# One step order in the first attention of a four-layer kernel: the second maximum behind the second scores

## What is computed

```python
x = layernorm(hidden_states) * ln_w + ln_b
q, k, v = x @ Wq + bq, x @ Wk + bk, x @ Wv + bv      # 16 heads of 8 channels
q, k = l2norm(q), l2norm(k)
state = q
for _ in range(2):
    att = softmax(einsum('bqhd,bkhd->bhqk', state, k))
    state = einsum('bhqk,bkhd->bqhd', att, v)
return hidden_states + state @ Wo + bo
```

## Time and profile before

| what | value |
|---|---|
| median of three runs | 1473.08 us |
| span of the profiled execution, first to last instruction | 1467.2 us |
| TensorE / VectorE / ScalarE / GpSimd busy over the span | 89% / 77% / 66% / 51% |
| first scores of k = 0 and of k = 63 start at | 42.97 and 469.35 us of the span |
| mean granted TensorE clock over the span | 0.954 |
| granted clock from 88.73 to 470 us | 0.99 |

### The profile page before, as it was taken

The page is one execution under the profiler, slowest core; times in us unless marked ns, Lnnn a source line. Parts: engine busy times, 40 slices in busy tenths (PEclk is TensorE's granted clock), DMA queues, the critical chain, the costliest instruction groups (busy, mean ns, idle before and its releaser), DMA issues. The chain is left out here.

```text
span 1467.2 us, 34194 instructions
## 1 busy us (share of the span) xinstructions
PE 1305.1 (89%) x12121; PEld 987.2 (67%) x12121; DVE 1130.4 (77%) x3054; ACT 969.6 (66%) x1498; POOL 751.3 (51%) x961
## 2 busy tenths in 40 slices
PE   2899999999998689899927999999999998699997
PEld 1566666666654367899915777777777776588886
DVE  5578889889875667899956888888888776567776
ACT  1688888888886447777723777777777777343441
POOL 4775665787852363799866455455444220101112
PEclk9899999999998779999958999999999999799999
DMA  6000000111111021122121111111111110134353
GB/s 234 18 23 20 22 20 20 28 32 28 31 36 30 8 80 32 56 73 73 58 87 51 49 47 48 46 48 47 49 46 38 39 42 18 26 92 116 80 129 82
DMA packets 84430, 77.20 MB, mean 53 GB/s; under 512 B 18224, under 2 KB 72240, under 8 KB 83888
## 3 DMA queue, kind: packets, MB, share of 16 engines
q1 hardware_dynamic: 80176, 66.73, 17.1%
q0 software_dynamic: 4096, 8.40, 2.0%
HBM read 36.26 MB, written 13.63 MB: 34 GB/s over the span
## 5 line engine op out<-in xcount | busy, mean ns | idle before, releaser
L541 ACT ACTIVATE a_p<-a_ps_s 128x1024 f32<-128x1024 f32 x256 | 258.3, 1031 | 25.1 <-PE a_ps_s L400 22.2
L651 DVE TENSOR_REDUCE a_qt<-a_ps_d 128x2 fp32r<-128x512 f32 x256 | 174.6, 687 | 48.9 <-PE a_ps_d L411 44.9
L1298 DVE TENSOR_REDUCE a_qt<-a_ps_d 128x2 fp32r<-128x512 f32 x256 | 173.3, 688 | 44.9 <-PE a_ps_d L1086 39.9
L822 POOL TENSOR_TENSOR a_rn<-a_ss,a_half 128x16 f32<-128x16 f32 x56 | 162.6, 2920 | 1.3
L1203 ACT ACTIVATE a_pg<-a_ps_s 128x1024 f32<-128x1024 f32 x128 | 125.8, 1024 | 26.8 <-PE a_ps_s L1075 25.4
L418 PE MATMUL a_ps_o<-a_p,a_v 128*32 128x256 f32 x2048 | 129.5, 393 | 3.7 <-ACT a_p L541 3.7
L1086 PE MATMUL a_ps_d<-a_kpad,a_qs 128*128 128x512 f32 x256 | 126.0, 495 | 5.8 <-DVE a_qt L1298 2.7
L411 PE MATMUL a_ps_d<-a_kpad,a_qs 128*128 128x512 f32 x256 | 126.8, 496 | 4.3 <-DVE a_qt L651 2.4
L2300 ACT ACTIVATE f_s<-f_ps_g 128x512 f32<-128x512 f32 x72 | 43.0, 598 | 99.9 <-PE f_ps_g L2246 99.7
L1494 POOL DMA_INDIRECT a_picked<-ys,rows x64 | 67.6, 1056 | 61.8 <-PE a_ps_d L1086 50.8
L418 PEld LDWEIGHTS a_ps_o<-a_p,a_v 128*32 128x32 f32 x2048 | 61.2, 112 | 52.9 <-issue 22.3
(11 more groups left out here) (355 smaller groups left out, 3823.9 us busy)
## 6 DMA issues: line engine op xcount, KB each, us to landing
a_kpad<-a_kc SPq DMA_DIRECT2D x512, 32.0 KB
f_gb<-spread SPq DMA_DIRECT2D x64, 256.0 KB, 5.7
a_kpad<-a_kq SPq DMA_DIRECT2D x256, 32.0 KB, 1.8
f_xin<-xs SPq DMA_DIRECT2D x39, 128.0 KB, 2.1
ys<-f_yout SPq DMA_DIRECT2D x39, 128.0 KB, 2.1
w<-in_w SPq DMA_DIRECT2D x2, 2304.0 KB, 11.4
out_x<-X SPq DMA_DIRECT2D x8, 256.0 KB, 6.8
xs<-f_zero SPq DMA_DIRECT2D x15, 128.0 KB
```

The lines of the kernel that those rows point to most:

```text
L541: nc.scalar.activation(probs[:, u % 2, 2 * c:2 * c + 2, :, :].rearrange("p a b c -> p (a b c)"), ps_s[:, 2 * c:2 * c + 2, :].rearrange("p ...
L651: nc.vector.tensor_reduce(qt2[:, (k - PEAK) % 4, 2 * part:2 * part + 2, SHIFT], bank(k, f"m{part}")[:, :].rearrange("p (a b) -> p a b", b= ...
L822: nc.gpsimd.tensor_tensor(rn[:, part * c:(part + 1) * c], ss[:, part * c:(part + 1) * c], half[:, 0:c], ALU.pow).then_inc(rn_ready, 1)
L1298: nc.vector.tensor_reduce(qt[:, b % 2, GLOBAL, n:n + 2, SHIFT], bank(k, f"m{part}")[:, :].rearrange("p (j s) -> p j s", s=S), AX.X, ALU.ma ...
```

## The change

In the first attention's steps the second scores move up directly behind the attend, ahead of qp and m1. m1 then stands next to m2. xT moves from r = 2 to r = 3, zT from r = 3 to r = 0 of the next batch (so that it serves the same sequences), and both now stand between yT and the attend, with their ScalarE copies between exp 0 and exp 1. The projections and the logits thereby use transposes of their own step. `D_ORDER` and VectorE's order stay as they are, and so do all other stages.

```diff
-    A_ORDER = ("yT", "xT", "T", "zT", "KQ")
+    A_ORDER = ("yT", "xT", "zT", "T", "KQ")
...
-                    "yT": r == 2 and batch(b - 2), "xT": r == 2 and batch(b + 3),
-                    "zT": r == 3 and 0 <= b - 3 < ROUTED}[task]
+                    "yT": r == 2 and batch(b - 2), "xT": r == 3 and batch(b + 3),
+                    "zT": r == 0 and 0 <= b - 4 < ROUTED}[task]
...
+                if a_live(k, "xT"):
+                    pe.wait_ge(z1_ready, b + 4)
+                    wait_a(st, "xT")
+                    transposes(ps_a, lambda t: z1[:, t, :], a_full)
+                if a_live(k, "zT"):
+                    pe.wait_ge(z_new, b - 3)
+                    wait_a(st, "zT")
+                    transposes(ps_a, lambda t: Z[:, ((b - 4) * TPB + t) * D:((b - 4) * TPB + t + 1) * D], a_full)
                 if unit(k - 1) or unit(k - LAST_USE):
...
                     last.then_inc(o_full, 1)
-                if a_live(k, "xT"):
-                    pe.wait_ge(z1_ready, b + 4)
-                    wait_a(st, "xT")
-                    transposes(ps_a, lambda t: z1[:, t, :], a_full)
-                if projects:
-                    pe.wait_ge(a_done, a_count(k - 1, "xT"))
-                    project(st, 0, "qp")
-                maxima(st, 1)
                 if unit(k - SECOND):
                     pe.wait_ge(exp_done, exps_of(k, 1))
                     pe.wait_ge(a_done, a_count(k - 1, "T"))
                     scores(k - SECOND, qs2[:, (k - 1) % 2, S:2 * S])
+                if projects:
+                    pe.wait_ge(a_done, a_count(k, "xT"))
+                    project(st, 0, "qp")
+                maxima(st, 1)
                 maxima(st, 2)
...
-                    pe.wait_ge(a_done, a_count(k - 1, "zT"))
+                    pe.wait_ge(a_done, a_count(k, "zT"))
...
-                if a_live(k, "zT"):
-                    pe.wait_ge(z_new, b - 2)
-                    wait_a(st, "zT")
-                    transposes(ps_a, lambda t: Z[:, ((b - 3) * TPB + t) * D:((b - 3) * TPB + t + 1) * D], a_full)
...
                 if a_live(k, "yT"):
                     copy_a(st, "yT", yT[:, :])
+                if a_live(k, "xT"):
+                    act.wait_ge(a_full, a_count(k, "xT"))
+                    nc.scalar.activation(xT[:, :], ps_a[:, 0:S], ACT.Identity, scale=a["ln_w"][:, 0:1],
+                                         bias=a["ln_b"][:, 0:1]).then_inc(a_done, 1)
+                if a_live(k, "zT"):
+                    copy_a(st, "zT", zT[:, :])
                 if unit(k):
                     exps(st, 1, k, p1)
...
-                        dve.wait_ge(a_full, a_count(k - NG, "xT"))
+                        dve.wait_ge(a_full, a_count(k - 3, "xT"))
```

More of the change, by code:

```diff
@@ L577, in _ @@
                     nc.scalar.copy(ot[:, live], ps_o[:, live]).then_inc(o_copied, 1)
[L578 to L581, removed]
                 if unit(k - SECOND):
@@ L588, in _ @@
                     exps(st, 3, k - SECOND, p2)
-                if a_live(k, "zT"):
-                    copy_a(st, "zT", zT[:, :])
                 if unit(k + NG):
```

## The result

The changed kernel takes 1479.12 us (median of 20 runs, 1471.41 to 1482.16) beside 1471.59 us for the kernel before (median of 20, 1468.0 to 1475.32): a ratio of 1.0046, interval 1.0035 to 1.0056, that is +6.8 us (5.1 to 8.2). The direction is the one forecast; the size is under half of the forecast +14.8, and the median lies 0.9 us under the range. The profiled execution has a span of 1476.0 us, 8.8 above that of before. The 1488 was 14.8 above a median of three runs, 1473.08; over twenty runs the kernel before has 1471.59, so 1.5 us of what 1488 was too high lie in that base.

A forecast was written before the change was run, and what follows sets the result against it. Two nearly equal loops, ScalarE's and the banks', were taken to bound the first attention. +13.1 (nine batches), +2.7 (b = 1 to 3) and -1.0 (routing steps) gave +14.8 on 1473.1: 1488 us, range 1480 to 1494.

The forecast's parts named there:

- two loops: Plain step of the first attention: ScalarE's loop closes at 6.30, the bank loop would at 5.92, 0.38 to spare.
- The rule on modes: TensorE in the first attention: one array turn fewer per step; by this alone the step would lose 0.10.
- rival B: First attention: TensorE's own issue is the bound, so the saved array turn makes it faster, -6, 1467; chance 0.06.
- routing steps: k = 31, and k = 47 in smaller measure: late for another reason, so 0.90 shrinks to about 0.15; 1.0 taken off.
- The step that failed most: r = 3: xT's copy holds exp 1 to 3.04, second scores at 3.19, qp 0.90 later; the step ends 0.90 later.
- the plain step: r = 1: m1 and m2 read in series, 0.68 each, O at 5.14, step 6.16 in place of 6.30, -0.14.
- 3 x (0.90 + 0.27 - 0.28): Batches b = 1 to 3, without lg: r = 3 and r = 2 cost, r = 0 and r = 1 gain; +2.7.
- The start ... and the last two batches: The 12 starting steps that wait for data and the last two batches, without projections: taken at nothing.
- m2's wait for qp's read: r = 3: m2 takes qp's bank, so TensorE stands until 4.94; from m2 to the step's end nothing gets shorter.
- A: Same places, half the size: r = 3 +0.67, yT not late, lg's lateness half absorbed; +8.8 less 1.0, 1481; chance 0.18.
- C: No change: r = 1's gain spreads to more steps, r = 3 half as bad; within 2.9 us of before; chance 0.05.
- D: Worse: VectorE's lateness carries on in routing steps and TensorE's idle costs granted clock; up to 6 more, 1494; chance 0.05.

The follow-up runs named there:

- experiment 7: The kernel before, with the second scores ahead of m1 in steps of r = 1 alone: ratio 0.9993 to the kernel before.
- experiments 9 and 10: VectorE's maxima over half of the keys, in the kernel before (ratio 0.9971) and in the changed kernel (0.9919), both to the same kernel before.
- Experiment 4: The changed kernel with qp alone moved ahead of the second scores, m1 behind them: ratio 1.0018 to the kernel before.
- Experiment 3: The changed kernel with the old order (qp, m1, second scores, m2) in steps of r = 3 only: ratio 0.9993 to the kernel before.
- experiment 8: Second scores early only without projections, lg, place and yT; xT in r = 3, zT at its old place, yT behind the attend: 1467.26 us beside 1471.39, ratio 0.9958.
- the control: The kernel before with VectorE's four maxima per step taken over the first 128 of each 256 keys: ratio 0.9971 to the kernel before.
- experiment 6: The changed kernel with the old order (m1, second scores, m2) in steps of r = 0 only, zT still ahead of the attend: ratio 1.0047 to the kernel before.

## Why the prediction was right in its sign and wrong in its size

**What held.** There are two loops, ScalarE's and that of the two banks, and the change shortens one and lengthens the other. The second scores stand behind the attend at 2.74; m1 and m2 follow one another 0.34 apart and are read in series; in r = 2 yT waits for the end of O's read (0.98 in, 0.97 forecast), and experiment 7 shows that wait arising from the order in r = 1 alone; in r = 0 lg waits for m1's read; in r = 3 qp starts 0.72 later than before and the step is 0.71 longer, since from m2 to its end it takes 3.54, as before (3.53). Three of the four step lengths came within 0.08: 6.72 (6.72), 6.08 (6.16), 6.99 (7.03). Nothing behind the stage changes but by what one execution differs from another.

**The rule on modes** doesn't decide it. The Trainium skill's page "TensorEngine Tiling (Array Packing)", Key Properties, says that a switch of the tiling mode drains the engine. The spacings agree with that: m1 and m2 are 0.34 apart without a turn between them, and were 0.43 from the second scores with one. But a turn fewer saves nothing while O waits for m2's read, and rival B falls with the sign of the result and with experiments 9 and 10.

**Where the 14.8 went.** Measured in the span: 8.8, so 6.0 less. By the stretches shown above:

| term | forecast | measured |
|---|---|---|
| ahead of k = 0 | 0 | -0.95 |
| b = 1 to 3, with the start (k = 0 to 15) | +2.7 | +1.24 |
| nine batches, per batch | 9 x 1.45 = +13.1 | 9 x 1.14 = +10.3 |
| their routing steps | -1.0 | -1.1 |
| k = 52 to 62 | 0 | -1.10 |
| from k = 63 on | 0 | +0.41 |

*The step that failed most* is the one on r = 3: "it holds the next exp for 0.54", "Exp 1 ends at 3.04, so the second scores go at 3.19". The copy of xT holds exp 1 for 0.45 only (306.25 to 306.70); exp 1 ends at 2.96, and the scores follow at 3.01, 0.05 behind it, and not 0.15. The 0.54 wasn't the price of a copy at all. In the earlier trace rows exp 2 waited for the second scores, whose row in k = 38 before is this:

```profile
295.80 0.51 PE L400 MATMUL a_ps_s<-a_qs,a_kq 32*128 32x256 f32 x8
```

Exp 2 stands 0.56 behind them, at 296.36, as it stands 0.56 behind them in the plain step (289.11 and 289.67) where no copy of xT lies between. The 0.15 is from the end of exp 3 to the next step's first scores. Wherever in this stage the first scores wait for an exp they start 0.14 to 0.15 behind its end, and wherever the second do, 0.05, in the kernel before too (k = 59, 440.63); why the two differ isn't known. All behind it moved with this error: qp 3.45 for 3.63, m2 4.75 for 4.94, the step 8.28 for 8.47. Over the 12 steps of this kind that is 2.3 us.

In the plain step the reads of m1 and m2 lie closer than the 0.68 that I took from three in a row, which gives O at 5.06 for 5.14 and the step 0.08 less. Over the nine batches that is 0.7 us; the plain steps of b = 1 don't get shorter (k = 4 takes 4.94 in both kernels, k = 5 5.89 in place of 5.72), which leaves 0.6. In r = 2 the forecast was 0.04 too high in each of the nine batches, and wrong in its kind in b = 1 and 2, where "3 x (0.90 + 0.27 - 0.28)" takes a late yT for granted: k = 6 has no finished batch to transpose, so it only loses xT (6.08 in place of 6.47), and k = 10 takes 6.83 in place of 6.77. With 0.04 in k = 14 that makes 1.3 us. Together 4.2 of the 6.0; the ends of the stage, below, are 2.0, and what follows k = 63 goes 0.4 the other way.

*"The start ... and the last two batches ... I take at nothing, their parts having both signs"* fails by 2.0 us. Ahead of k = 0 the stacks no longer stand behind xT, which waits for tokens: -0.95. And in steps without projections, zT in r = 3 was no cover for waits but a wait itself. Before, in k = 59, it stands at 442.84 behind 0.60 of idle that ScalarE's copy of T ends; O waits behind it, 5.84 into the step, and its own copy on ScalarE then holds the stacks to 444.03, 6.78 in. The rows are these:

```profile
442.84 0.41 PE L431 MATMUL a_ps_a<-ident,Z 128*128 128x128 f32 x2 [0.60 <-ACT a_qs L547]
443.09 0.60 PE L524 MATMUL a_ps_d<-ident,a_ot 128*128 128x128 f32 x4
444.03 0.41 PE L425 MATMUL a_ps_a<-ident,a_kt 128*128 128x128 f32 x2 [0.34 <-ACT a_zT L547]
```

With zT gone to r = 0, O stands at 5.35 and the stacks, held by nothing, at 5.85: the step takes 6.38 in place of 7.34, and k = 55 6.68 in place of 7.48. Both gains could have been read from the trace of before.

*The routing steps* gave the sum that was taken, by other parts: k = 31 8.29 (8.33 before; +0.15 forecast, -0.04 measured), k = 47 8.27 (7.78), but k = 33 and 49, where place stands between m2 and m3, 7.30 in place of 7.07, while a plain step gains. Place waits there for m1's read (0.21 of idle at 266.53 in k = 33), 0.24 later than before. That the sum agreed is chance.

**m2's wait for qp's read** was seen as forecast, but it isn't the only path, as I had it. Experiment 4 takes it away and gets 0.13 of the 0.71. Experiment 3 gives 0.48 to the scores ahead of qp and m1, and 0.23 to xT ahead of the attend. In the changed kernel two paths lead from qp's read, which ends at 4.69, and they tie: m2 starts at 4.75 and can be read 0.54 later, at 5.29; and m1's read, which starts behind qp's on VectorE at 4.61 and takes 0.68, ends at 5.29 too. In experiment 4 qp is early, but m1 has followed the second scores and isn't read before 4.55, m2's read comes behind it, and kp behind that.

**The rivals.** A gave 1481, the nearest to 1479, and rightly had r = 3 at +0.67 (measured +0.71); but its other two parts, yT not late and lg's wait halved, didn't come, so that its total is near by luck: the ends of the stage, which it has at nothing too, made up for them. B fell with the sign. C needed three steps wrong at once, and r = 3 alone, at +0.71, speaks against it; D's loss of granted clock didn't come (1.00 in the steps shown), but its lateness where place stands between m2 and m3 did, by 0.23 in k = 33 and 49.

## What to carry to other kernels

Where products go in turn into two shared banks, price a new order kind of step by kind of step: write down when each read starts with the reads in series, and follow which product waits for it; one order can gain 0.22 in a plain step and cost 0.71 in a loaded one, and then the order is best chosen for each kind (experiment 8: 0.9958, where the change for all steps gives 1.0046). Don't book the ends of a pipeline at nothing: work that covers waits in the full steps is on the path where the cover is gone. And take a latency from a row of the same two instructions, one waiting for the other: from an exp's end to the first scores it is 0.15 here and to the second 0.05, and the distance from a copy to the exp behind it is the copy's price only where that exp waits for nothing else.

## What the runs showed that was not expected

- The part of the program behind k = 63, the same code throughout, took 985.4 to 1003.2 us in the profiled executions of this study. A change of a few us in the first stage is read from its steps, and not from one span.
- A 128x256 copy between two exps costs 0.45 from start to start (306.25 to 306.70). The 0.54 of the earlier trace rows is no such price: that exp starts when the second scores allow it.
- A maximum over half the elements (128x256 in place of 128x512) takes 0.42 in place of 0.69 us.
- Step k = 62 takes 12.0 us before and 12.3 after with full reads, at a granted clock of 0.77, and 6.5 and 6.3 with short ones, at 1.00 in the control.
- In experiment 6's execution k = 59, 60 and 61 had a granted clock of 0.86, 0.92 and 0.78, with TensorE idle in them. The edit is far from those steps; this stays open.
